# New places for all stages of a four-layer graph network in the engines' instruction lists

## What is computed

```
x = layer0(x, adj)   # 8-head attention, scores masked by adj + eye, out @ Wo, x + out, layer norm
x = layer1(x, adj)   # 8-head attention, scores + gate terms + log(adj + 1e-9), x + out
x = layer2(x, adj)   # feat = x @ W_fc + b; leaky_relu(q + k^T, masked by adj); softmax; att @ feat + x
x = layer3(x, adj)   # 8-head attention, scores + log(clip(adj)), out @ Wo, x + out, layer norm
```

## Time and profile before

| | us |
|---|---|
| median of 3 runs (lowest, highest) | 1841.31 (1839.12, 1843.48) |
| the profiled execution, its own time | 1840.3 |
| its span, first to last instruction | 1838.4 |
| PE busy in the span | 1731.4 |
| DVE busy | 1483.9 |
| POOL busy | 1269.3 |
| ACT busy | 1214.8 |

### The profile page before, as it was taken

How to read it: one execution, slowest core, us unless ns; L and a number is a source line. 1 busy time by engine, 2 the same in 40 slices (tenths; PEclk the granted TensorE clock), 3 DMA queues, 4 the chain that set the end, 5 groups by cost and what they waited for, 6 DMA issues and landing times.

```text
span 1838.4 us, 54870 instructions
## 1 busy us (share of the span) xinstructions
PE 1731.4 (94%) x23564; PEld 1321.4 (72%) x23564; DVE 1483.9 (81%) x3008; ACT 1214.8 (66%) x1894; POOL 1269.3 (69%) x903
## 2 busy tenths in 40 slices
PE   5999998899999999889999999989999999998996
PEld 4677776777777777677777777767777777767774
DVE  5899877777799977877789987787779998777775
ACT  3567765567777676456776777546777676754675
POOL 4443898288964489638895459945888446992788
PEclk8999999999999999999999999999999999999998
DMA  6100010001120000100221000010112100011011
GB/s 166 36 30 13 19 37 25 24 25 53 49 75 19 19 19 31 47 2 25 60 75 43 24 19 19 25 46 8 42 53 71 42 19 18 15 36 35 14 30 36
DMA packets 67734, 66.46 MB, mean 36 GB/s; under 512 B 6051, under 2 KB 67493, under 8 KB 67493
## 3 DMA queue, kind: packets, MB, share of 16 engines
q1 hardware_dynamic: 66388, 62.16, 11.3%
q10 hardware_dynamic: 1104, 0.79, 0.1%
HBM read 54.54 MB, written 8.39 MB: 34 GB/s over the span
## 4 chain that ended last, share of the span: by engine, by line
PE 77%; DVE 17%; ACT 2%; issue 1%; POOL 1%; SPq 1%; DMA 1%; DVEq 0%; POOLq 0%; ACTq 0%
PE gx L609 23%; PE od L747 17%; PE sc L714 17%; PE gx L760 6%; PE gx L634 3%; PE sc L708 3%; PE sc L720 3%; DVE ring L999 3%; PE gx L796 3%; DVE qk L950 2%; PE gx L727 2%; DVE lg L1043 2%; DVE negm L972 1%; DVE parts L972 1%; DVE parts L975 1%
## 5 line engine op out<-in xcount | busy, mean ns | idle before, releaser
L594 POOL TENSOR_TENSOR ring<-ring,adj_c 128x1024 f32<-128x1024 f32 x256 | 609.4, 2406 | 107.7 <-ACT ring L865 55.1
L714 PE MATMUL sc<-qk 32*128 32x256 f32 x9216 | 410.8, 294 | 11.0 <-ACT m_rows L853 4.4
L714 PEld LDWEIGHTS sc<-qk 32*128 32x128 f32 x9216 | 320.5, 184 | 109.3 <-issue 62.7
L850 ACT ACTIVATE aside<-sc 128x1024 f32<-128x1024 f32 x192 | 196.6, 1024 | 232.4 <-PE sc L714 152.7
L865 ACT ACTIVATE ring<-sc 128x1024 f32<-128x1024 f32 x256 | 248.4, 1023 | 29.8 <-PE sc L720 29.3
L569 POOL TENSOR_TENSOR xs<-xs,bo 128x512 f32<-128x512 f32 x96 | 128.3, 1337 | 182.7 <-DVE xt_lo L942 163.5
L747 PE MATMUL od<-ring,vf 128*32 128x256 f32 x3072 | 243.9, 389 | 3.1 <-POOL ring L594 3.1
L747 PE MATMUL od<-ring,ones_r 128*32 128x256 f32 x3072 | 236.7, 380 | 0.0
L972 DVE TENSOR_REDUCE parts<-sc 128x4 f32<-128x1024 f32 x128 | 155.8, 1217 | 50.2 <-PE sc L714 49.5
L999 DVE TENSOR_TENSOR ring<-ring,adj_c 128x1024 f32<-128x1024 f32 x128 | 177.6, 1429 | 0.0
L863 ACT ACTIVATE ring<-sc,vf 128x1024 f32<-128x1024 f32 x128 | 135.8, 1113 | 36.5 <-PE sc L720 36.4
(11 more groups left out here) (146 smaller groups left out, 4433.5 us busy)
## 6 DMA issues: line engine op xcount, KB each, us to landing
adj_c<-in_adj_t SPq DMA_DIRECT2D x96, 256.0 KB, 2.8
...
```

The costliest lines, as they stand in the source:

```text
L594: pool.tensor_tensor(part, part, adj_c[i.mi % 3][:, t, :].unsqueeze(1).to_broadcast([P, G, N]), ALU.mult).then_inc(weighted, 1)
L714: mm = pe.matmul(sc[:, g, t * N:(t + 1) * N], buf[rows, a, c, t * P:(t + 1) * P], buf[rows, b, c, :], start=(n == 0 and not masked), stop= ...
L850: act.activation(aside[:], sc[:, 0:2, :], ACT.Copy).then_inc(set_aside, 1)
```

## The change

Only the tables change. Of PE's 1536 list entries 822 stand at another position, by at most 7; of ACT's 1129 650; of the 1225 that DVE acts on 541; of POOL's 480 364; of SP's 224 157, by at most 9. No instruction is added or taken away, and the 124 loads of ACT's function tables that the order implies stay 124. The lists of one item in the middle of each layer, sorted out of the tables (a stage, its half, a point, the item), before and after:

The diff:

```diff
--- before.py
+++ after.py
@@ -41,88 +41,88 @@
 
 PE, ACTE, DVE, POOL, SP = "pe", "act", "dve", "pool", "sp"
 MHA_PLAN0 = {
-    "T": {PE: [-1.369], ACTE: [-0.812], DVE: [-0.531]},
-    "Q": {PE: [0.448], ACTE: [0.62], DVE: [0.618]},
-    "P": {PE: [0.898], ACTE: [1.182], DVE: [1.37]},
-    "V": {PE: [1.755], ACTE: [2.169], DVE: [-6.493]},
-    "S": {PE: [3.78, 5.523], ACTE: [3.928, 5.676], DVE: [4.321, 5.732]},
-    "U": {DVE: [6.726]},
-    "M": {PE: [8.077], ACTE: [8.609]},
-    "E": {PE: [8.732, 10.486], ACTE: [8.916, 10.799], POOL: [6.877, 7.831], DVE: [10.96, 12.555]},
-    "A": {PE: [13.457, 13.547, 15.008, 15.85]},
-    "N": {DVE: [14.694, 16.472]},
-    "F": {PE: [18.521]},
-    "XB": {POOL: [-2.308]},
-    "H": {DVE: [19.057]},
-    "LC": {SP: [-3.406]},
-    "PC": {POOL: [1.774]},
+    "T": {PE: [-1.435], ACTE: [-1.788], DVE: [-2.502]},
+    "Q": {PE: [0.621], ACTE: [-0.282], DVE: [0.175]},
+    "P": {PE: [1.121], ACTE: [0.752], DVE: [0.655]},
+    "V": {PE: [1.871], ACTE: [1.496], DVE: [-32.097]},
+    "S": {PE: [3.796, 5.239], ACTE: [2.953, 4.956], DVE: [2.343, 4.802]},
+    "U": {DVE: [5.396]},
+    "M": {PE: [7.866], ACTE: [7.489]},
+    "E": {PE: [8.624, 10.115], ACTE: [8.2, 9.568], POOL: [-5.602, -3.552], DVE: [9.191, 11.776]},
+    "A": {PE: [12.906, 13.376, 14.229, 14.634]},
+    "N": {DVE: [12.822, 14.828]},
+    "F": {PE: [18.376]},
+    "XB": {POOL: [-18.108]},
+    "H": {DVE: [17.498]},
+    "LC": {SP: [-17.341]},
+    "PC": {POOL: [-14.379]},
 }
 MHA_PLAN1 = {
-    "O": {POOL: [3.4]},
-    "T": {PE: [-1.478], ACTE: [-0.654], DVE: [-0.835]},
-    "Q": {PE: [0.325], ACTE: [0.792], DVE: [0.506]},
-    "P": {PE: [0.888], ACTE: [1.261], DVE: [0.856]},
-    "V": {PE: [2.152], ACTE: [2.533], DVE: [-5.843]},
-    "S": {PE: [4.069, 5.361], ACTE: [4.042, 6.06], DVE: [3.914, 6.094]},
-    "U": {DVE: [7.002]},
-    "M": {PE: [8.263], ACTE: [8.128]},
-    "E": {PE: [8.458, 10.289], ACTE: [9.016, 10.771], POOL: [8.893, 10.747], DVE: [11.927, 12.772]},
-    "A": {PE: [13.219, 14.013, 15.503, 15.976]},
-    "N": {DVE: [14.184, 16.686]},
-    "F": {PE: [18.326]},
-    "XB": {POOL: [3.878]},
-    "H": {DVE: [19.026]},
-    "LC": {SP: [-3.627]},
-    "PC": {POOL: [6.782]},
+    "O": {POOL: [-13.829]},
+    "T": {PE: [-1.509], ACTE: [-2.184], DVE: [-2.089]},
+    "Q": {PE: [0.4], ACTE: [0.095], DVE: [-0.743]},
+    "P": {PE: [1.048], ACTE: [0.429], DVE: [-0.209]},
+    "V": {PE: [1.958], ACTE: [1.117], DVE: [-27.681]},
+    "S": {PE: [3.108, 5.088], ACTE: [2.819, 4.487], DVE: [2.727, 4.216]},
+    "U": {DVE: [4.94]},
+    "M": {PE: [8.2], ACTE: [7.596]},
+    "E": {PE: [10.209, 12.572], ACTE: [9.681, 12.253], POOL: [-6.132, -5.244], DVE: [26.456, 28.45]},
+    "A": {PE: [15.038, 15.08, 16.701, 16.941]},
+    "N": {DVE: [14.851, 15.715]},
+    "F": {PE: [18.47]},
+    "XB": {POOL: [-11.79]},
+    "H": {DVE: [17.296]},
+    "LC": {SP: [0.441]},
+    "PC": {POOL: [-12.037]},
 }
 MHA_PLAN3 = {
-    "T": {PE: [-1.19], ACTE: [-1.073], DVE: [-0.698]},
-    "Q": {PE: [0.636], ACTE: [0.369], DVE: [1.202]},
-    "P": {PE: [1.218], ACTE: [1.533], DVE: [2.181]},
-    "V": {PE: [5.67], ACTE: [6.124], DVE: [-9.553]},
-    "S": {PE: [3.514, 5.371], ACTE: [4.002, 5.553], DVE: [4.205, 5.767]},
-    "U": {DVE: [6.406]},
-    "M": {PE: [7.81], ACTE: [8.254]},
-    "E": {PE: [8.642, 10.048], ACTE: [8.758, 10.82], POOL: [7.379, 7.824], DVE: [4.208, 7.121]},
-    "A": {PE: [11.495, 12.869, 14.21, 14.607]},
-    "N": {DVE: [13.302, 15.208]},
-    "F": {PE: [19.244]},
-    "XB": {POOL: [-1.681]},
-    "H": {DVE: [19.215]},
-    "LC": {SP: [1.4]},
-    "PC": {POOL: [0.247]},
+    "T": {PE: [-1.34], ACTE: [-1.791], DVE: [-2.279]},
+    "Q": {PE: [1], ACTE: [-0.352], DVE: [-0.562]},
+    "P": {PE: [1.976], ACTE: [1.77], DVE: [1.062]},
+    "V": {PE: [5.313], ACTE: [5.477], DVE: [-39.841]},
+    "S": {PE: [4.299, 5.779], ACTE: [3.576, 5.209], DVE: [3.083, 4.874]},
+    "U": {DVE: [5.315]},
+    "M": {PE: [8.46], ACTE: [7.617]},
+    "E": {PE: [9.016, 10.213], ACTE: [7.823, 9.871], POOL: [-12.771, -10.801], DVE: [-13.004, -11.717]},
+    "A": {PE: [11.21, 13.118, 14.742, 14.954]},
+    "N": {DVE: [12.514, 15.218]},
+    "F": {PE: [18.562]},
+    "XB": {POOL: [-22.445]},
+    "H": {DVE: [17.994]},
+    "LC": {SP: [-24.173]},
+    "PC": {POOL: [-18.097]},
 }
 LN_PLAN0 = {
-    "B": {DVE: [20.521]},
-    "Z": {ACTE: [21.887]},
-    "Y": {DVE: [27.099], ACTE: [28.749], POOL: [28.572]},
+    "B": {DVE: [18.234]},
+    "Z": {ACTE: [20.965]},
+    "Y": {DVE: [24.252], ACTE: [26.72], POOL: [10.682]},
 }
 LN_PLAN3 = {
-    "B": {DVE: [19.777]},
-    "Z": {ACTE: [22.008]},
-    "Y": {DVE: [23.028], ACTE: [25.306], POOL: [23.757]},
+    "B": {DVE: [18.264]},
+    "Z": {ACTE: [21.156]},
+    "Y": {DVE: [21.417], ACTE: [22.923], POOL: [2.052]},
 }
 FIRST_PLAN = {
-    "LX": {SP: [-5.633]},
-    "LR": {SP: [-11.454]},
-    "PR": {POOL: [-3.015]},
+    "LX": {SP: [-31.037]},
+    "LR": {SP: [-37.348]},
+    "PR": {POOL: [-24.396]},
 }
 LAST_PLAN = {
-    "OUT": {SP: [24]},
+    "OUT": {SP: [0.406]},
 }
 GAT_PLAN = {
-    "T": {PE: [-1.283], ACTE: [-1.168], DVE: [-0.48]},
-    "G": {PE: [0.327, 0.617], DVE: [0.68, 0.921]},
-    "J": {ACTE: [1.277]},
-    "K": {PE: [6.757]},
-    "L": {DVE: [7.376]},
-    "X": {ACTE: [8.099]},
-    "W": {PE: [11.782], ACTE: [11.913]},
-    "C": {DVE: [13.038], PE: [12.846]},
-    "LR": {SP: [11.922]},
-    "PR": {POOL: [0.713]},
+    "T": {PE: [-1.152], ACTE: [-1.887], DVE: [-2.432]},
+    "G": {PE: [-0.062, 1.675], DVE: [-1.062, 1.963]},
+    "J": {ACTE: [3.153]},
+    "K": {PE: [7.529]},
+    "L": {DVE: [6.89]},
+    "X": {ACTE: [8.774]},
+    "W": {PE: [12.491], ACTE: [11.809]},
+    "C": {DVE: [12.364], PE: [14.052]},
+    "LR": {SP: [-17.028]},
+    "PR": {POOL: [-18.461]},
 }
-PITCH = {0: (4, 4), 1: (4, 4), 2: (4.5, 4.5), 3: (4, 4)}
+PITCH = {0: (4, 4), 1: (4, 4), 2: (4.75, 4.75), 3: (4, 4)}
 GAT_START, LAST_START = 24, 33.5
```

## The result

| | before | after |
|---|---|---|
| median of 4 runs (lowest to highest), us | 1842.39 (1839.12 to 1843.71) | 1828.86 (1827.13 to 1831.54) |
| the profiled execution: time, span | 1840.3, 1838.4 | 1827.72, 1825.9 |

The ratio is 0.993 (95% interval 0.9911 to 0.995): 13.5 us faster, where 29 were forecast. The time lies inside the range of 1796 to 1835, but less than half of the forecast gain came.

The account below looks back on a forecast made before the run. PE, busy 94% of the span, bounds the kernel and idles mainly at layer borders, start and end. 4 x (5.1 + 1.7 + 1.6 - 0.4 - 1.0) + 3.5 - 2.5 = 29.0 us gained: 1812, range 1796 to 1835.

Parts of the forecast that it names:

- Layer 0 to 1: Border where E0.72 moves behind V.74: the 3.26 us wait and the half clock behind it go; 5.1 us gained a group.
- Layer 1 to 2: Border where PE reaches T.80 3.0 us earlier and POOL's last product ends 1 us earlier; 1.7 us gained a group.
- Start: Kernel start, once: DVE's late copies delay S0.0, and Q.1 follows at about 32 us; 2.5 us lost, between 0 and 5.
- A new order can win nothing there, because the matmuls stay the same: Inside the blocks of one layer, where PE is full at clock 1.00, reordering gains 0.
- tight V: Layer 1: V.77 follows P.77 with only S1 between, next to no slack for the buffer; 0.4 us lost a group.
- Layer 2 to 3: Border where T.90's 1.45 us wait goes because it needs V.88's buffer, not P.89's; T.91 1.6 us earlier a group.
- The sign that the prediction named: Border from layer 2 to 3 in the changed profile: T.91 would come 1.6 us closer to T.88.
- end: Kernel end, once: F.126 moves ahead of A2.127, into the wait for POOL; 3.5 us gained, between 1 and 5.
- less than feared: Layer 0: POOL's PC and XB meet DVE's E0 masks, costing DVE 0.7 to 2.1 us an item; PE 1.0 a group.
- (a): Rival at the borders: the POOL and DVE collision moves but stays; only 10 us gained, 1831 us; chance 0.18.
- (b): Rival in layer 0: DVE's masks meet POOL throughout, items over 17.8 us; slower, 1849 us; chance 0.09.
- (c): Rival: gains at one border are given back at the next because POOL sets the pace; 1838 to 1845 us; chance 0.06.

Follow-up runs that it names:

- the run on the kernel before: Kernel before, PE's list only: A0 ahead of P in layer 0, A1 directly behind A0 in late layer-1 items; 1839.81 us, ratio 0.9989.

## Why the prediction was half right

**Layer 0 to 1, right (20.4 forecast, 17.4 came).** POOL's products for E0.72 beside DVE's masks of E1.71 were the cause of V.74's wait. After, no L999 takes over 2.30, V.74 waits for nothing, and the clock stays at 1.00 at all four borders. Moving E0.72 alone gave 9.4 of the 17.4 there (4.3 of idle time, 5.1 of clock), as 2.2 of the 3.26 a group came back at P.74, E1.72 and S0.74. The other 8.0 came from the rest of the new order at this border, which no run takes apart. The prediction booked 4.6 a group for the first part and 0.5 for the rest, and they brought 2.35 and 2.0: the sum came out nearer than its terms. The idle time that stays (1.05 a group) is mostly 0.80 at P.74. It was right that the half clock belongs to the wait; it was not said that another wait can take it over.

**Layer 1 to 2, the step that failed (+1.7 forecast, -1.8 a group came).** The prediction took an arrival of PE 3.0 us earlier and an end of POOL's last product 1 us earlier, and booked 1.7 between them; the wait behind L1048 was to stay as it is. What sets the border is neither of the two but DVE: L.80 ahead of T.82 in its list, slowed by POOL. Against L1048 PE arrived 0.75 sooner (1.59 us behind its start in place of 2.34), so the wait grew from 1.73 to 2.19, and half clock followed in three groups. Moving T.82 and PE's list with it brought 10.6 us, leaving out the product 11.1. The error is one of method: the wait at G0.82 was in the rows, with its releaser, and the sum was made from other engines' ends.

**Start (-2.5 forecast, -7.5 came).** The late copies were seen, and Q.1 at about 32 was named; it came at 35.82. The 3.8 between them come from the half clock: S0.0, 5.2 us in the kernel before, took 9.6 behind the wait of 7.34, and the estimate left only the old duration for it. The other 1.2 of the miss stay open.

**"A new order can win nothing there, because the matmuls stay the same", wrong (0 forecast, +8.2 came).** Two stages A that follow each other take 0.13 to 0.14 less than two apart. The list of after has 259 runs of A in place of 301; at that price 42 fewer runs are 5.9 of the 8.2. In layer 0, P is more often followed by S1, whose first matmuls are masks in P's own tile form, and not by an A: S stands directly behind an A in 29 places instead of 47, and at 0.11 each, by the layer-0 item of the run on the kernel before, that is 2.0. Together 7.9 of 8.2. Shown by runs: 4.1 less on the kernel before by both means, 3.2 less by joining in layer 0 of after, 2.4 more by parting in its layer 3. Busy did not mean fixed: the stretch was full in both kernels.

**Layer 1 (-1.6 forecast, -4.0 came).** The tight V of the prediction was not it: Z.71, with two table loads of 1.28, stands ahead of E0.74 on ACT.

**Layer 2 to 3 (+6.4 forecast, +1.3 came).** T.90's wait of 1.45 went, and W.87, which took over the buffer of P.89, has one of 1.49. With W.87 out of the way S0.89 waits 1.40: the chain is P.89, its low part on DVE, then S0.89, whoever takes the buffer. The sign that the prediction named misleads here: T.91 did come 1.3 closer to T.88 (31.85 to 30.53), but 0.5 of waiting now stands directly behind T.91, at S0.90.

**Layer 2, layer 3, layer 0, end.** 6.0 an item, as said. In layer 0 the masks meet less than feared: DVE's busy time in the item rises by 0.7 (16.38 to 17.10), the low end of the forecast, the item takes 17.41, and idle time is 0.6 more in all. At the end F.126 runs under POOL's last products, and only F.127 stands behind A3.127, as said; but part of the 5.0 is luck. The 5.46 of the two F were at half clock (3.81 in the kernel with E0.72 moved, at full clock), so 2.9 of the 5.0 is clock that no longer falls on matmuls, and that kernel's end is 2.6 shorter with no change in its lists there.

**The rivals.** (a) was the nearest in its sum, 1831, and in its kind: a collision that stays and moves the wait. (b) did not occur; items of 17.41 rule it out. Of (c), what is won at one border and given back at the next, 7.2 of 17.4 us came true, but the pace was DVE's and not POOL's.
